# A gated cross-attention and transformer block with experts on one core: head operands placed by selection matmuls, 32-row tiles, and all cross-attention slots before the self-attention

## What is computed

```python
x = x + tanh(g_xattn) * cross_attention(layernorm(x), ctx_768)   # 512 keys per sequence, one head
x = x + tanh(g_ffn)   * block(layernorm(x))
# block(X), X is 4 x 256 x 128:
h = rmsnorm(X, norm1_w)
q, k, v = h @ wq, h @ wk, h @ wv                 # 16 heads of 8 features
X = X + (softmax(q k^T / sqrt(8)) v) @ wo        # self-attention, per head 256 x 256
h2 = rmsnorm(X, norm2_w)
combine = top-2 of softmax(h2 @ router_w)        # 8 experts
out = X + swiglu_shared(h2) + sum_e combine_e * swiglu_e(h2)   # all 8 experts computed densely
```

## Time and profile before

| what | value |
|---|---|
| median of 3 runs | 249.85 us (249.34 to 250.36) |
| the profiled execution: its time | 249.14 us |
| the profiled execution: its span, first to last instruction | 247.4 us |
| mean granted TensorE clock | 0.922 of 2.4 GHz |
| TensorE (PE) busy | 202.7 us, 82% of the span |
| VectorE (DVE) busy | 152.5 us, 62% |
| ScalarE (ACT) busy | 101.3 us, 41% |
| GpSimd (POOL) busy | 58.8 us, 24% |
| DMA packets | 7124, 12.83 MB |

### The profile page before, as it was taken

One profiled execution on the slowest core, in us unless ns is written; L12 is line 12 of the kernel. 1 busy time (PEld: TensorE's weight loads), 2 busy tenths in 40 slices (PEclk: granted clock), 3 DMA queues, 4 the chain that ended last, 5 costly groups with the idle time before them and its releaser, 6 DMA issues.

```text
span 247.4 us, 3838 instructions
## 1 busy us (share of the span) xinstructions
PE 202.7 (82%) x1327; PEld 161.2 (65%) x1327; DVE 152.5 (62%) x393; ACT 101.3 (41%) x203; POOL 58.8 (24%) x77
## 2 busy tenths in 40 slices
PE   7699695659783798299888577899789999999994
PEld 5467464446572566167665455688668888888883
DVE  3779999647653175446687642478874654655653
ACT  8153265930162274246584565423231221221320
POOL 8566969310140020011011011003302332000000
PEclk9999998865679599869999999999979999999999
DMA  6900002535934023400000010000002230000002
GB/s 175 269 0 4 0 16 72 153 104 121 229 103 105 7 90 85 91 3 5 9 1 5 3 48 0 3 0 0 4 0 64 87 107 0 21 3 1 1 3 85
DMA packets 7124, 12.83 MB, mean 52 GB/s; under 512 B 992, under 2 KB 4576, under 8 KB 6592
## 3 DMA queue, kind: packets, MB, share of 16 engines
q1 hardware_dynamic: 7104, 12.58, 19.1%
HBM read 9.69 MB, written 2.62 MB: 50 GB/s over the span
## 4 chain that ended last, share of the span: by engine, by line
PE 48%; DVE 19%; DMA 12%; SPq 11%; issue 3%; ACT 3%; POOL 2%; DVEq 0%; ACTq 0%; POOLq 0%
PE bank L1066 12%; PE bank L1083 7%; PE bank L1085 6%; PE bank L1084 6%; DMA split_scratch<-split 5%; DMA q_st<-negmT 5%; PE bank L1052 5%; SPq L320 4%; SPq L323 4%; PE bank L1037 4%; PE bank L1026 3%; DVE mxs L822 2%; DVE xs L696 1%; DVE small L703 1%; DVE y L690 1%
## 5 line engine op out<-in xcount | busy, mean ns | idle before, releaser
L822 DVE TENSOR_REDUCE mxs<-bank 128x2 f32<-128x512 f32 x64 | 42.5, 689 | 27.9 <-PE bank L1026 27.4
L588 ACT ACTIVATE ep<-bank 128x512 f32<-128x512 f32 x64 | 37.5, 595 | 35.3 <-PE bank L1037 34.7
L1037 PE MATMUL bank<-q_st,k_st 128*128 128x256 f32 x128 | 28.8, 311 | 16.7 <-DMA q_st<-negmT 13.3
L1026 PE MATMUL bank<-k_st,q_st 128*128 128x256 f32 x128 | 34.3, 363 | 2.2 <-DVE mxs L822 1.1
L1066 PEld LDWEIGHTS bank<-down_s,vx 128*128 128x128 f32 x288 | 34.9, 193 | 1.8 <-issue 0.4
L1066 PE MATMUL bank<-down_s,vx 128*128 128x128 f32 x288 | 35.2, 276 | 0.0
L612 ACT ACTIVATE silu<-bank 128x512 f32<-128x512 f32 x28 | 16.6, 598 | 43.9 <-PE bank L1085 43.9
L1037 PEld LDWEIGHTS bank<-q_st,k_st 128*128 128x128 f32 x128 | 21.9, 210 | 18.5 <-DMA q_st<-negmT 13.9
L1083 PE MATMUL bank<-h2hi,whi 128*128 128x512 f32 x72 | 30.8, 428 | 2.7 <-ACT silu L612 2.7
L1026 PEld LDWEIGHTS bank<-k_st,q_st 128*128 128x128 f32 x128 | 23.5, 231 | 10.5 <-issue 4.5
L1085 PE MATMUL bank<-h2hi,wlo 128*128 128x512 f32 x72 | 29.1, 404 | 0.0
(11 more groups left out here) (139 smaller groups left out, 288.4 us busy)
## 6 DMA issues: line engine op xcount, KB each, us to landing
raw<-expert_w SPq DMA_DIRECT2D x9, 256.0 KB, 3.7
split_scratch<-split SPq DMA_DIRECT2D x16, 128.0 KB, 2.2
q_st<-split_scratch SPq DMA_DIRECT2D x16, 128.0 KB
k_st<-split_scratch SPq DMA_DIRECT2D x16, 128.0 KB
down_s<-expert_w SPq DMA_DIRECT2D x9, 128.0 KB, 2.7
ctxT<-ctx_T SPq DMA_DIRECT2D x1, 672.0 KB, 7.7
xs<-x_tiles SPq DMA_DIRECT2D x2, 256.0 KB, 4.2
out_dram<-x SPq DMA_DIRECT2D x2, 256.0 KB, 2.0
```

Of the source, the lines that this page charges most:

```text
L588: nc.scalar.activation(ep[:, n % NEP].rearrange("p t s -> p (t s)"), b_of(("exp", n))[:], ACT.Exp, scale=SCALE_H).then_inc(free(("exp", n) ...
L822: nc.vector.tensor_reduce(mxs[:, n // NH, :, n % NH], b_of(("max", n))[:].rearrange("p (t s) -> p t s", t=TB), AX_X, ALU.max).then_inc(fre ...
L1026: last = pe.matmul(b_of(("max", n))[:, j * L:(j + 1) * L], q_st[:, b % NSTACK, h // 2, j * P:(j + 1) * P], k_st[:, b % NSTACK, k_slot(h), ...
L1037: last = pe.matmul(b_of(("exp", n))[:, j * L:(j + 1) * L], k_st[:, b % NSTACK, k_slot(h), j * P:(j + 1) * P], q_st[:, b % NSTACK, h // 2, ...
```

## The change

- The scratch tensor, `stack`, `place_m`, `clear_pads`, `copy_picks` and the three-fold `q_st` and `k_st` are gone. Instead each sequence has a `q4` and a `k4` of 128 partitions: four heads with 32 rows each, four groups. They are filled by **selection matmuls**: in a new step of an x slot (SEL_AT = 7, so x slots 7, 9, 11 and 13) TensorE multiplies the split q and k with 0/1 matrices `sel`, 16 matmuls of 256 columns into four bank uses (`stq` 0 and 1, `stk` 0 and 1); ScalarE reads the two of q, VectorE the two of k.
- The score products work on **32-row tiles** (`tile_position=(r, 0)`), two heads at a time in two row groups and two banks. A pair of heads takes one even slot, where one head took each slot. The negated maximum is no longer in the operand: a matmul of 512 columns per head (`pick` times `negm`) opens the exp bank and the two score matmuls add to it.
- Every a slot stands behind the last x slot (A_FROM = 14 = the number of x slots). LAG is 12, the misc steps stand one slot earlier.
- NEARLY is 8: eight items stand among the a slots, every second slot from 62 and every slot from 76 on. All nine experts' weights stay in the memory, so no load waits for an item; SP issues all expert loads at the beginning.
- `ep` has 8 places instead of 6.

```diff
-LAG = 13
+LAG = 12
-M_STEPS = [("mT0", 8, 8), ("mT1", 17, 17)]
-C_STEPS = [("uT0", 31, 31), ("uT1", 32, 32), ("cT", 34, 34), ("wo", 36, 36), ("square", 37, 37), ("h2", 38, 38),
-           ("h2T", 41, 41), ("router", 43, 43)]
-A_FROM = 10
-A_PER_X = 6
-M_FROM = 68
+M_STEPS = [("mT0", 8, 8), ("mT1", 16, 16)]
+C_STEPS = [("uT0", 30, 30), ("uT1", 31, 31), ("cT", 33, 33), ("wo", 35, 35), ("square", 36, 36), ("h2", 37, 37),
+           ("h2T", 40, 40), ("router", 42, 42)]
+A_FROM = 14
+A_PER_X = 3
+M_FROM = 62
 M_EVERY = 2
-T_FROM = 80
-T_EVERY = 2
-NEARLY = 4
+T_FROM = 76
+T_EVERY = 1
+NEARLY = 8
+SEL_AT = 7
-NEP = 6
+NEP = 8
...
-            stack(sp, 0)
-            stack(sp, 1)
-            for e in range(NRAW, NSPLIT):
-                load_expert(sp, e)
-            place_m(sp, 0, 0)
-            stack(sp, 2)
...
-            for e in range(NSPLIT, NEXP):
+            for e in range(NEXP):
                 load_expert(sp, e)
...
# GpSimd
-            clear_pads(1)
             norm2(1)
-            clear_pads(2)
...
             for b in range(NB):
                 norm3(b)
                 split_h2(b)
+                for e in range(4 + 2 * b, min(6 + 2 * b, NEXP)):
+                    split_weights(e)
...
# ScalarE, x_slot (VectorE has the same with stk and k4)
+                b = sequence_at(slot, SEL_AT)
+                if b is not None:
+                    for part in range(2):
+                        use = ("stq", b, part)
+                        is_full(act, use)
+                        nc.scalar.copy(q4[:, b, 2 * part:2 * part + 2, :].rearrange("p g s -> p (g s)"),
+                                       b_of(use)[:]).then_inc(free(use), 1)
...
# TensorE, x_slot
+                b = sequence_at(slot, SEL_AT)
+                if b is not None:
+                    if b == 0:
+                        pe.wait_ge(sel_ready, 4)
+                    pe.wait_ge(hi_ready, b + 1)
+                    is_read(pe, ("qk2", b))
+                    for qk, name in ((0, "stq"), (1, "stk")):
+                        for part in range(2):
+                            use = (name, b, part)
+                            may_fill(pe, use)
+                            for g in range(2):
+                                for hl in range(2):
+                                    last = pe.matmul(b_of(use)[:, g * L:(g + 1) * L], sel[:, qk, hl, 2 * part + g, :],
+                                                     split[:, b % 2, hl, qk, :], start=(hl == 0), stop=(hl == 1))
+                            last.then_inc(full(use), 1)
...
# TensorE, a_slot
-                n = slot
-                if n < NHEADS:
...
-                    for j in range(TB):
-                        last = pe.matmul(b_of(("max", n))[:, j * L:(j + 1) * L],
-                                         q_st[:, b % NSTACK, h // 2, j * P:(j + 1) * P],
-                                         k_st[:, b % NSTACK, k_slot(h), :], start=True, stop=True)
-                    last.then_inc(full(("max", n)), 1)
+                if slot < NHEADS and slot % 2 == 0:
...
+                    may_fill(pe, ("max", slot))
+                    may_fill(pe, ("max", slot + 1))
+                    for j in range(TB):
+                        for o in range(2):
+                            r, use = 32 * ((h + o) % 4), ("max", slot + o)
+                            last = pe.matmul(b_of(use)[:, j * L:(j + 1) * L],
+                                             q4[r:r + 32, b, h // 4, j * P:(j + 1) * P], k4[r:r + 32, b, h // 4, :],
+                                             start=True, stop=True, tile_position=(r, 0))
+                            if j == TB - 1:
+                                last.then_inc(full(use), 1)
                 n = slot - LAG
...
-                        pe.wait_ge(m_placed[2 * b + h // 8], 16)
+                        written(("mT", b, half))
                     may_fill(pe, ("exp", n))
...
+                    may_fill(pe, ("exp", n + 1))
+                    for o in range(2):
+                        r = 32 * ((h + o) % 4)
+                        pe.matmul(b_of(("exp", n + o))[:].rearrange("p (t s) -> p t s", t=TB), pick[r:r + 32, h // 4 % 2, :],
+                                  negm[r:r + 32, half, :].unsqueeze(1).broadcast_to([32, TB, L]),
+                                  start=True, stop=False, tile_position=(r, 0))
+                    for j in range(TB):
+                        for o in range(2):
+                            r, use = 32 * ((h + o) % 4), ("exp", n + o)
+                            last = pe.matmul(b_of(use)[:, j * L:(j + 1) * L],
+                                             k4[r:r + 32, b, h // 4, j * P:(j + 1) * P], q4[r:r + 32, b, h // 4, :],
+                                             start=False, stop=(j == TB - 1), tile_position=(r, 0))
```

236 lines of the change are left out of this document (93 added, 143 removed).

## The result

| | kernel before | with the change |
|---|---|---|
| median of the runs | 249.59 us (248.62 to 250.36, four runs) | 267.15 us (265.2 to 270.38, four runs) |
| ratio | | 1.068 (95% interval 1.0602 to 1.0757) |
| span of the profiled execution | 247.4 us | 264.9 us |
| mean granted clock | 0.922 | 0.836 |

A forecast was written before the change was run, and what follows sets the result against it. It took chained x slots, then DMA waits with slow stretches among the heads, then TensorE as bounds. Stage terms 57.4 + 12.3 + 2 + 59.0 + 10.4 + 22.7 + 33 + 53.4 gave 250.2 us of span, forecast 252.5; range 243 to 262.

The forecast's parts named there:

- The clock stays low among the heads: Rival: TensorE stays at 1.2 GHz among the heads, four slots some 6.3 us, total 278 us; chance 0.06.
- the term of slots 12 to 60: Heads with everything: 12 x 4.1 + 2 x 4.9 = 59.0 us, plus 2 us for a first low-clock stretch.
- the last stage: From the eighth down projection to the end of the span, ten items with the table load: 53.4 us.
- The price of a pair: TensorE's matmuls for two heads, bound by weight loads: 0.43 us for maxima, 0.64 us for exp scores with picks.
- the first rival: Row tiles overlap in full: 0.25 + 0.50 us a pair, four slots 3.5 us, total 244 us; chance 0.27.
- The walk through four slots: Pair, product with the values, pair: 4.1 us where 3.63 was measured, as TensorE waits for VectorE's two reads.
- The x slots: Stage before the heads: third projection at about 46.9 us, fourth from 52.3, first maxima at 57.4, before 53.5.
- selection chains of the last two sequences: New x-slot step of selection matmuls and copies, a pure chain with nothing else beside it: 3.4 us each.
- The pairs of the first slots: Slots 0 to 12, maxima alone: 6 pairs x 2.05 = 12.3 us, TensorE at half the clock.
- Slots 60 to the eighth down projection: Last heads with early thirds, three terms: 10.4 us, 22.7 us and 33 us.
- The wait at `uT0`: Misc step where TensorE waits for ScalarE's copy, now behind two exps instead of one: +0.6 us.
- the later start of the heads: The heads start behind all x slots, with first maxima at 57.4 instead of 53.5 us: 4 us later.

The follow-up runs named there:

- e6: The kernel before, with both score products cut to rows 0 to 31 as one 32-row tile; 281.72 us, ratio 1.123.
- e5: The change with all 128 rows in score products and picks, no tile position, so four heads are summed; 261.42 us, ratio 1.042 to before.
- e14: The change with all 128 rows in scores and picks (heads summed) and a pair's heads one by one; 244.74 us, ratio 0.976 to before.
- e4: The change with heads (a slots) from x slot 8 on instead of 14; 260.43 us, ratio 1.037 to before.
- e13: The change with all 128 rows in scores and picks (heads summed) and heads from x slot 8 on; 255.25 us, ratio 1.016 to before.
- e15: The change with whole rows (heads summed), a pair's heads one by one, and heads from x slot 8 on; 239.84 us, ratio 0.957 to before.
- e16: e15 made to compute the reference: q and k each kept twice with half of the heads' rows zeroed; 246.23 us, ratio 0.985 to before.
- e7: The kernel before, with both score products cut to rows 0 to 63 as a 64-row tile; 280.45 us, ratio 1.120.
- e9: The kernel before, with both score products cut to 72 rows and no tile position; 252.71 us, ratio 1.011.
- e1: The change plus one unused 512-column matmul on all 128 rows ahead of each pair's picks; 287.03 us, ratio 1.12 to before from one run.
- e11: The change with only the picks on all 128 rows, six ep places, and heads from x slot 8 on; 276.34 us, ratio 1.095 to before.
- e3: The change with a pair's heads one after the other in both score products, each waiting for its own bank; 262.15 us, ratio 1.045 to before.

## Why the prediction was wrong

**The step that failed** is the chance of 0.06 for "The clock stays low among the heads", and the sentence that carried it: "TensorE is then busy all the time, and under such load it came back within 4 us after each stall". The evidence for it was a stretch of whole-array matmuls. It says nothing of one in which the scores address 32-row tiles, and e6 shows such a stretch, 10.00 us of 10 busy, at 0.50. In the sum it is the term of slots 12 to 60: four slots at the price of the high clock, 12 x 4.1 + 2 x 4.9 + 2 = 61 us, measured 78.65. The mechanism that I had as a rival, at 278 us, is the one that ruled. Its price of 6.3 us for four slots measured 5.93. Of the 11 us by which it was too high, 8 stand in these slots, where TensorE was near the high clock three times for 3 to 6 us (0.95 to 0.97 from 78.96 to 82, 106 to 111 and 133.2 to 139 us), and 3 in the last stage.

**The price of a pair** was wrong in the other direction. I took the weight loads as the bound, 0.43 and 0.64 us. At the high clock the pair's maxima took 134.14 - 133.80 = 0.34 us with the change of tiling, its picks 0.24 for two of 512 columns, and all of it 134.71 - 133.80 = 0.91 us. I had 1.07, the first rival 0.75 without any change of tiling. The loads' records are long (twenty loads of L987 from 110 to 128 us, nearly all at half the clock):

```profile
L987 PEld LDWEIGHTS bank<-k,q 32*128 32x128 f32 x20 | 2.4, 282 | 5.2 <-DVE mxs L766 2.8 <-issue 2.4
...
L970 PEld LDWEIGHTS bank<-router_pad,probs 128*128 128x128 f32 x4 | 0.9, 322 | 0.2 <-issue 0.2
```

A load of 32 rows is 12% shorter than one of 128 rows, 282 against 322 ns. Four of 282 ns in a row would take 1.13 us, but a pair's four maxima with their loads took 90.41 - 89.81 = 0.60 at that clock, so loads of different tiles lie beside each other. The Trainium skill has both halves ("TensorE: Matmul & The Clock Gate", section LDWEIGHTS, for the length; "TensorEngine Tiling (Array Packing)", Key Properties, for tiles that load in parallel), and the trace agrees with the second, and with the first to these 12%; I had let the first bound the pair.

**The walk through four slots** gave 4.1 us from the tie of a pair to VectorE. The tie is real: 9.0 us over slots 12 to 60 at the high clock (e5 against e14). In the change at the low clock it is little, 0.62 us in four slots. In its first short stretch at the high clock it is in full, although the tiles overlap:

```profile
78.96 0.57 PE L987 MATMUL bank<-k,q 32*128 32x256 f32 x4
...
81.00 0.50 PE L987 MATMUL bank<-k,q 32*128 32x256 f32 x4 [0.99 <-DVE mxs L766]
```

From pair to pair are 2.04 us, of which TensorE waits 0.99. Twice this is 4.1 us for four slots, an estimate from these two rows, where the first rival had 1.67 + 1.85 = 3.5.

**What came out.** The x slots: third projection at 45.27 for 46.9, fourth at 52.02 for 52.3, selection chains of the last two sequences 3.6 and 3.5 us for 3.4, first maxima at 57.16 for 57.4. The last is partly luck: the third projection came 1.6 us early, and the fourth 6.75 us behind it instead of 5.4, because two normalising steps (1.88 us, beside GpSimd's split of an expert) stood ahead of VectorE's split of the third. TensorE's timeline there:

```profile
52.02 1.10 PE L901 MATMUL bank<-xnT,ffn_s 128*128 128x256 f32 x4 [0.39 <-DVE k L676]
54.62 1.18 PE L921 MATMUL bank<-split,sel 128*128 128x256 f32 x8 [1.05 <-DVE split L668]
56.00 1.23 PE L921 MATMUL bank<-split,sel 128*128 128x256 f32 x8 [0.20 <-ACT q L472]
57.16 0.50 PE L987 MATMUL bank<-k,q 32*128 32x256 f32 x4
59.41 0.50 PE L987 MATMUL bank<-k,q 32*128 32x256 f32 x4 [1.75 <-DVE mxs L766]
```

The pairs of the first slots are 59.41 - 57.16 = 2.25 us apart at first, 2.05 forecast. No TensorE wait on a DMA is left among the heads. Slots 60 to the eighth down projection: 65.89 for 66.1; its three terms weren't measured one by one. The wait at `uT0` is 1.44 us each time (98.83 above). The last stage was 3.0 us shorter than forecast, mainly because TensorE's wait for the first silu behind the table load is 0.25 us now:

```profile
216.74 0.47 PE L1057 MATMUL bank<-h2hi,whi 128*128 128x512 f32 x1 [0.25 <-ACT silu L540]
```

In the kernel before it was 2.68 us, and behind it stood a stretch at 0.65 (181.6 to 186.5 us), which is gone too. A new wait of 0.91 us at 218.58 takes a part back.

**The gain that the change did bring** is real and was spent: both long DMA waits are gone. In e14, whole rows and single heads but the change's order, slots 12 to 60 take 60.71 us against 65.79 before. That this meets my 61 is luck: e14 has no tie of pairs, and pays for picks over all rows instead.

**The order** costs 4.5 to 6.7 us (e4, e13, e15, e16 against their twins). I had priced the later start of the heads at 4 us. It doesn't end there: in slots 0 to 12 only VectorE's maxima count, and in the change from 60 to 70 us TensorE was busy 3.51 us of 10 and granted 0.60, then 0.54 from 70 to 80. With x slots among the first heads e15 was granted 1.00 from 57 to 75 us, e14 without them 0.81.

**What stays open.** Which property of a row-tiled stretch keeps the clock down isn't told apart further than e6, e7 and e9 do, nor what lifts it among row tiles, as from 120 us on in e1, from 113 in e11 and, among the early thirds, from 172 in the change. The product with the values addresses 32-column tiles in every kernel here and didn't keep it down. No run holds row tiles at the high clock over all the heads without added work, so what the change would take then is not shown.

## What to carry to other kernels

Price a change of tiling at both clock levels and read the granted clock of the stretch: overlap of small tiles that halves the matmul time gained nothing here, as the clock fell to half for everything around it. Where an operand can be padded with zeros to whole rows, try that version beside the tiled one before anything else is tuned. When two limits lie over each other, removing one alone shows little (5.0 us for single heads, 5.7 us for whole rows); run the pair of edits before calling either small (22.4 us together).

## What the hardware showed that was not expected

- With its scores on row tiles TensorE stood at its low level of 1.2 GHz under full load: 0.50 for 20 us with 20.00 us busy (e6), and 280 to 282 us for the kernel before with 32- or 64-row tiles, 252.7 with 72 rows and no tile (0.50 there too from 70 to 100 us).
- One matmul of 512 columns on the whole array for each pair of heads didn't bring the clock back for 40 us (e1: 0.50 at 90% busy, 80 to 120 us), and then it stood at 0.94 for 30 us among the same tiles.
- Two 32-row tiles overlap in full: two picks of 512 columns in 0.24 us at the high clock and 0.43 at the low one. Heads issued one after the other overlap as well (e3, 0.98 us for 1.7).
- In the change the clock was high three times for 3 to 6 us among the heads. Twice it came up 4 to 6 us behind eight whole-array transposes of probabilities, and was low again at the maxima behind TensorE's next long wait for VectorE, 2.59 us long at 113.49 and 2.51 at 141.44.
